# Cross-attention: keys, values and queries projected with tokens on partitions

## What is computed

```
q = layernorm(x) @ Wq + bq;  k = ctx @ Wk + bk;  v = ctx @ Wv + bv      # 256 -> 32 = 8 heads x 4
attn = softmax(q k^T * scale) per head;  o = attn v
x = x + tanh(g_xattn) * (o @ Wo + bo)
logits = layernorm(x) @ router_w + router_b;  scores = softmax(logits)  # 8 experts
per expert: the 512 tokens with the highest scores; relu(tok @ w1 + b1) @ w2 + b2, times score, added back
x = x + tanh(g_ffn) * (that sum)
```

## Time and profile before

| | |
|---|---|
| median of 3 runs | 587.21 us (587.1 to 587.39) |
| the profiled execution | 587.2 us, span 585.4 us |
| TensorE (PE) busy | 549.5 us, 94% |
| VectorE (DVE) | 443.0 us, 76% |
| ScalarE (ACT) | 389.7 us, 67% |
| GpSimd (POOL) | 215.3 us, 37% |

### The profile page before, as it was taken

One profiled execution on the slowest core, in us unless ns is written; L12 is line 12 of the kernel. 1 busy time (PEld: TensorE's weight loads), 2 busy tenths in 40 slices (PEclk: granted clock), 3 DMA queues, 4 the chain that ended last, 5 costly groups with the idle time before them and its releaser, 6 DMA issues.

```text
span 585.4 us, 12822 instructions
## 1 busy us (share of the span) xinstructions
PE 549.5 (94%) x5043; PEld 320.0 (55%) x5043; DVE 443.0 (76%) x811; ACT 389.7 (67%) x762; POOL 215.3 (37%) x205
## 2 busy tenths in 40 slices
PE   7799999999999999999999988899999999999994
PEld 3433333333343333433334444479889898898973
DVE  3889989998899878999895277655866858676541
ACT  1577878988789887898889820055665556555651
POOL 3057175001835018300157110231544625447234
PEclk9999999999999999999999999999999999999998
DMA  8700000000000000000000104113634646356133
GB/s 279 248 2 1 1 1 3 2 1 38 2 37 2 2 38 1 38 2 2 37 38 2 38 19 163 31 50 100 146 108 109 166 133 136 109 109 168 14 36 36
DMA packets 23808, 35.80 MB, mean 61 GB/s; under 512 B 3460, under 2 KB 16197, under 8 KB 23621
## 3 DMA queue, kind: packets, MB, share of 16 engines
q1 hardware_dynamic: 17604, 26.59, 13.9%
q0 software_dynamic: 6144, 8.39, 8.1%
HBM read 26.59 MB, written 8.39 MB: 60 GB/s over the span
## 4 chain that ended last, share of the span: by engine, by line
PE 71%; DVE 17%; ACT 4%; issue 4%; POOL 1%; DMA 1%; POOLq 0%; DVEq 0%; ACTq 0%; SPq 0%
PE ps L1744 15%; PE ps L1751 15%; PE ps L1515 13%; DVE mquart L1040 10%; PE ps L1481 7%; PE ps L1502 6%; ACT probs L767 2%; PE ps L1411 2%; PE ps L1372 2%; PE ps L1387 1%; PE ps L1722 1%; PE ps L1697 1%; ACT osb L666 1%; PE ps L1540 1%; POOL out L636 1%
## 5 line engine op out<-in xcount | busy, mean ns | idle before, releaser
L1040 DVE TENSOR_REDUCE mquart<-ps 128x2 f32<-128x802 f32 x256 | 240.1, 988 | 25.8 <-PE ps L1481 23.7
L767 ACT ACTIVATE probs<-ps 128x512 f32<-128x512 f32 (+1 forms) x416 | 223.4, 595 | 27.6 <-PE ps L1502 25.0
L1515 PE MATMUL ps<-probs,vp 128*32 128x256 f32 (+1 forms) x1664 | 132.7, 391 | 4.2 <-ACT osb L666 4.0
L1481 PE MATMUL ps<-kpad,qrows 64*128 64x401 bf16 x512 | 89.5, 337 | 5.5 <-DVE mquart L1040 5.2
L1502 PE MATMUL ps<-qfull,kpad 64*128 64x256 bf16 (+1 forms) x832 | 88.6, 272 | 1.6 <-ACT x L788 1.4
L1340 DVE TENSOR_TENSOR h1l<-hf,h1h 128x512 fp32r<-128x512 f32 x64 | 44.3, 692 | 56.0 <-ACT hf L892 48.0
L891 ACT ACTIVATE h1h<-ps,b1T 128x512 fp32r<-128x512 f32 x64 | 43.9, 686 | 54.3 <-PE ps L1744 52.5
L1751 PE MATMUL ps<-w2h,h1h 128*128 128x256 f32 x256 | 73.8, 288 | 2.1 <-DVE h1l L1340 1.5
L1751 PE MATMUL ps<-w2l,h1h 128*128 128x256 f32 x256 | 72.4, 283 | 0.0
L1751 PE MATMUL ps<-w2h,h1l 128*128 128x256 f32 x256 | 72.3, 283 | 0.0
L636 POOL DMA_INDIRECT out<-eo,idx_put x32 | 55.2, 1726 | 26.2 <-ACT eo L901 17.0
(11 more groups left out here) (200 smaller groups left out, 696.1 us busy)
## 6 DMA issues: line engine op xcount, KB each, us to landing
w1raw<-in_L_ffn_w SPq DMA_DIRECT2D x16, 512.0 KB, 4.6
w2raw<-in_L_ffn_w SPq DMA_DIRECT2D x16, 512.0 KB
xs<-in_x SPq DMA_DIRECT2D x4, 512.0 KB, 7.5
ctx_sb<-in_ctx SPq DMA_DIRECT2D x3, 512.0 KB, 5.8
out<-xs SPq DMA_DIRECT2D x3, 512.0 KB, 2.7
x_rows<-x SPq DMA_DIRECT2D x3, 512.0 KB, 2.6
b2b<-in_L_ffn_b SPq DMA_DIRECT2D x1, 1024.0 KB, 11.3
out<-xs SPq DMA_DIRECT2D x2, 256.0 KB, 2.0
```

What stands on the lines that cost most here:

```text
L767: nc.scalar.activation(out_p, ps[0:w, next_bank(), :], ACT.Exp, scale=float(SCALE)).then_inc(s_ex, 1)
L1040: nc.vector.tensor_reduce(mquart[:, u % 2, t, a, :, kq], ps[:, b:b + 2, 0:MAXW], AX.X, ALU.max).then_inc(s_mr, 1)
L1481: last = mm(ps[:, bank + b, 0:MAXW], qrows[band(b), g, q:q + P], kpad[band(b), g, a, lo:lo + MAXW], start=True, stop=True)
L1515: last = mm(ps[32 * hh:32 * hh + 32, PV, 0:UW], vp[0:w, kt, g, hh, :], probs[0:w, step % PROBS, hh, :], start=(kt == 0), stop=(kt == NKT - 1))
```

## The change

The f32 weights for keys and values lie side by side (`wkv_sb`, 64 columns). `project_kv` takes 128 context tokens as weights of the array and the 64 columns as moving data, so keys and values come out with tokens on partitions, for both groups at once; the bias is one product of a row of ones. ScalarE copies k and v to `kvsb` and writes the high part into two slots of `ktok` (`keys_high`), VectorE writes middle and low (`keys_split`), GpSimd the third high one and the values into `vp` (`high_again`). `turn_keys` multiplies a tile of `ktok` with the identity in bf16, which turns it to rows; the padded copies are made straight from PSUM (`pad_k0` by VectorE for blocks 0, 2, 3, by ScalarE for block 1; `pad_k1` by ScalarE).

For queries: `project_q`, then the split in `qtok` (by VectorE for chunk 0 in `first_queries`, by GpSimd for later chunks), `turn_q` for each group, and a copy to `qrows`. Per chunk there is one projection at (1, 3) and turns at (1, 7) and (1, 9). `max_parts` writes its two parts into `qtok` itself, and `place_max` turns `qtok` once more, maxima included, without the product that copied the rows. Replicated weights, bias products, four keep-busy products and the transposes of values go.

```diff
+KV_BANKS, TURN_BANKS, Q_BANK, QT_BANK = (4, 5, 4, 5), (2, 6, 2, 1), 3, 0
+kparts = ktok[:, :, :, :].rearrange("p n g (h j d) -> p (n g h) j d", j=8, d=HD)
+qparts = [qtok[:, i, :, :, :].rearrange("p t g (h j d) -> p (t g h) j d", j=8, d=HD) for i in range(2)]
+HEADS = CT * NH
...
-XN_FIRST, XN_LATER, Q_AT = ((0, 7), (0, 9)), ((0, 0), (0, 3)), ((1, 3), (1, 7))
+XN_FIRST, XN_LATER, Q_AT, ROWS_AT = ((0, 7), (0, 9)), ((0, 0), (0, 3)), (1, 3), ((1, 7), (1, 9))
...
-FIRST_VALUES, FIRST_KEYS, FIRST_QUERIES = (2, 6, 10, 13), (3, 7), 11
...
+FIRST_KEYS, FIRST_QUERIES = (1, 3, 5, 7), 9
...
-    for t, w in ((wk_sb, Wk), (wq_sb, Wq), (wv_sb, Wv)):
-        sp.dma_start(t[:, :, :], w.rearrange("(k p) n -> p k n", p=P)).then_inc(s_wts, 16)
+    for t, w in ((wkv_sb[:, :, 0:32], Wk), (wkv_sb[:, :, 32:64], Wv), (wq_sb[:, :, :], Wq)):
...
-    nc.gpsimd.memset(wqr[:, :, :, :], 0.0)
-    nc.gpsimd.memset(wkr[:, :, :, :], 0.0)
-    nc.gpsimd.memset(bqkr[:, :, :], 0.0).then_inc(s_zero, 1)
-    nc.gpsimd.memset(mparts[:, :, :, :], 0.0).then_inc(s_zero, 1)
+    nc.gpsimd.memset(ktok[:, :, :, :], 0.0).then_inc(s_zero, 1)
+    pool.wait_ge(s_zero, 1)
+    nc.gpsimd.memset(kparts[:, :, KROW_M // HD, 0:2], 1.0).then_inc(s_zero, 1)
+    nc.gpsimd.memset(qtok[:, :, :, :, :], 0.0).then_inc(s_zero, 1)
     nc.gpsimd.memset(vp[:, :, :, :, :], 0.0).then_inc(s_zero, 1)
-    pool.wait_ge(s_zero, 3)
+    pool.wait_ge(s_zero, 4)
...
+    def high_again(j):
+        ms, w = keys_of(j), block_rows(j)[1]
+        pool.wait_ge(s_khi, j + 1)
+        nc.gpsimd.tensor_copy(kparts[0:w, ms, 5, :], kparts[0:w, ms, 0, :]).then_inc(s_kh5, 1)
+        pool.wait_ge(s_zero, 5)
+        nc.gpsimd.tensor_copy(vp[:, :, :, :, :].rearrange("p k g h d -> p (k g h) d")[0:w, ms, 0:HD],
+                              kvsb[0:w, j % 2, P:P + 32 * (ms.stop - ms.start) // NH].rearrange("p (m d) -> p m d", d=HD)).then_inc(s_vp, 1)
...
-    for b, (lo, w) in enumerate(KB):
...
-    split_rest(pool, nc.gpsimd, 9, 1, CW)
-    split_rows(pool, nc.gpsimd, 9, CW, qrows[:, 1, 0:CW])
+    for j in range(4):
+        high_again(j)
...
-    def split_queries(c, g, n):
...
+    def split_queries(c):
+        parts, q = qparts[c % 2], qsb[:, :].rearrange("p (m d) -> p m d", d=HD)
+        rest = qres[:, :].rearrange("p (m d) -> p m d", d=HD)
+        pool.wait_ge(s_qtk, c)
+        if c > 1:
+            pool.wait_ge(s_mpl, PER_CHUNK * (c - 1))
+            nc.gpsimd.memset(parts[:, :, KROW_M // HD, 0:2], 0.0)
+        nc.gpsimd.tensor_copy(parts[:, :, 0:2, :], q.unsqueeze(2).to_broadcast([P, HEADS, 2, HD])).then_inc(s_qhi, 1)
+        pool.wait_ge(s_qhi, c)
+        nc.gpsimd.tensor_tensor(rest, q, parts[:, :, 0, :], ALU.subtract).then_inc(s_qrest, 1)
+        nc.gpsimd.tensor_copy(parts[:, :, 4, :], q)
+        pool.wait_ge(s_qrest, c)
+        nc.gpsimd.tensor_copy(parts[:, :, 2:4, :], rest.unsqueeze(2).to_broadcast([P, HEADS, 2, HD])).then_inc(s_qmid, 1)
+        pool.wait_ge(s_qmid, c)
+        nc.gpsimd.tensor_tensor(parts[:, :, 5, :], rest, parts[:, :, 2, :], ALU.subtract).then_inc(s_qd, 1)
...
-    def qk_bias(n, half, kind, g, w, bank, s_ready, cnt_ready):
...
+    def keys_high(j):
+        (tiles, w), ms = block_rows(j), keys_of(j)
+        act.wait_ge(s_kv, j + 1)
+        act.wait_ge(s_zero, 2)
+        if j > 1:
+            act.wait_ge(s_ktok, j - 1)
+            act.wait_ge(s_vp, j - 1)
+        nc.scalar.activation(kvsb[0:w, j % 2, :].rearrange("p (x c) -> p x c", x=2)[:, :, 0:32 * tiles],
+                             ps[0:w, KV_BANKS[j], 0:2 * P].rearrange("p (x c) -> p x c", x=2)[:, :, 0:32 * tiles], ACT.Copy)
+        nc.scalar.activation(kparts[0:w, ms, 0:4:2, :],
+                             ps[0:w, KV_BANKS[j], 0:32 * tiles].rearrange("p (m d) -> p m d", d=HD).unsqueeze(2).to_broadcast([w, NH * tiles, 2, HD]),
+                             ACT.Copy).then_inc(s_khi, 1)
+    def pad_k0(j):
+        lo, w = KB[j]
+        act.wait_ge(s_kt, j + 1)
+        for b in range(2):
+            last = nc.scalar.activation(kpad[:, 0, b, lo:lo + w], ps[:, TURN_BANKS[j], 0:w], ACT.Copy,
+                                        scale=cst[:, C_HEAD + b:C_HEAD + b + 1])
+        last.then_inc(s_ka, 1)
+    def take_q(c, g, bank):
+        act.wait_ge(s_qt, NG * c + g + 1)
+        take(qrows[:, g, CW * c:CW * c + CW], ps[:, bank, :], s_qr)
...
     take_ctx(0)
     take_ctx(1)
-    act.wait_ge(s_bias, 1)
-    bias_k(0)
+    keys_high(0)
     take_ctx(2)
-    bias_k(1)
-    take_v(0, 0)
+    keys_high(1)
     take_ctx(3)
-    bias_k(2)
     for k in range(KD):
         act.wait_ge(s_T, k + 1)
         take(xnT[:, k, :], ps[:, XN_BANKS[k], :], s_Tt)
-    take_v(1, 0)
-    bias_k(3)
-    qk_bias(4, 2, "q", 0, CW, JOB, s_Q, 1)
-    take_v(2, 0)
-    take_v(3, 0)
+    keys_high(2)
+    keys_high(3)
+    pad_k0(1)
+    take_q(0, 0, QT_BANK)
...
-        qk_bias(5 + j, (5 + j) % 2, "k", 1, KB[j][1], next_bank(), s_kp, 4 + j + 1)
...
+        pad_k1(j, next_bank())
+    take_q(0, 1, next_bank())
+    def take_q_tokens(c, bank):
+        act.wait_ge(s_Q, c + 1)
+        at_least(act, s_qd, c - 1)
+        take(qsb[:, :], ps[:, bank, 0:CW // HD], s_qtk)
...
-    for w, r in ((wk_sb, wkr), (wq_sb, wqr)):
...
-    def split(n, half, w, mask, dst):
...
     def keys_split(j):
+        (tiles, w), ms = block_rows(j), keys_of(j)
+        k, rest = [a.rearrange("p (m d) -> p m d", d=HD) for a in (kvsb[0:w, j % 2, 0:32 * tiles], kres[0:w, 0:32 * tiles])]
+        dve.wait_ge(s_khi, j + 1)
+        at_least(dve, s_ktok, j)
+        link(nc.vector.tensor_tensor(rest, k, kparts[0:w, ms, 0, :], ALU.subtract))
+        link(nc.vector.tensor_copy(kparts[0:w, ms, 1:5:2, :], rest.unsqueeze(2).to_broadcast([w, NH * tiles, 2, HD])))
+        nc.vector.tensor_tensor(kparts[0:w, ms, 4, :], rest, kparts[0:w, ms, 1, :], ALU.subtract).then_inc(s_ktok, 1)
+    def pad_k0(j):
         lo, w = KB[j]
-        split(j, j % 2, w, 2, krows[:, j % 2, 0:w])
-        dve.wait_ge(s_rows, j + 1)
+        dve.wait_ge(s_kt, j + 1)
         for b in range(2):
-            last = nc.vector.tensor_scalar(kpad[:, 0, b, lo:lo + w], krows[:, j % 2, 0:w],
-                                           cst[:, C_HEAD + b:C_HEAD + b + 1], None, ALU.mult)
-        last.then_inc(s_kpad0, 1)
+            last = nc.vector.tensor_scalar(kpad[:, 0, b, lo:lo + w], ps[:, TURN_BANKS[j], 0:w], cst[:, C_HEAD + b:C_HEAD + b + 1], None, ALU.mult)
+        last.then_inc(s_kd, 1)
+    def first_queries():
+        q, rest = [a.rearrange("p (m d) -> p m d", d=HD) for a in (ps[:, Q_BANK, 0:CW // HD], qres[:, :])]
+        parts = qparts[0]
+        dve.wait_ge(s_Q, 1)
+        link(nc.vector.tensor_copy(parts[:, :, 0:2, :], q.unsqueeze(2).to_broadcast([P, HEADS, 2, HD])))
+        link(nc.vector.tensor_tensor(rest, q, parts[:, :, 0, :], ALU.subtract))
+        nc.vector.tensor_copy(parts[:, :, 4, :], parts[:, :, 0, :])
+        link(nc.vector.tensor_copy(parts[:, :, 2:4, :], rest.unsqueeze(2).to_broadcast([P, HEADS, 2, HD])))
+        nc.vector.tensor_tensor(parts[:, :, 5, :], rest, parts[:, :, 2, :], ALU.subtract).then_inc(s_q0, 1)
     take_ctx(0)
     for t in range(CT):
         ln1_stats(0, t)
     take_ctx(1)
     ln1_aggr(0)
+    keys_split(0)
     take_ctx(2)
-    keys_split(0)
     ln1_apply_first()
+    keys_split(1)
     take_ctx(3)
-    keys_split(1)
+    pad_k0(0)
     keys_split(2)
     keys_split(3)
-    split(4, 2, CW, 0, qrows[:, 0, 0:CW])
+    first_queries()
+    pad_k0(2)
+    pad_k0(3)
...
-        at_least(dve, s_mpl, u)
-        def spread(t, row):
-            return t[:, :, :, row].rearrange("p t (b a) -> p t a b", a=2)
-        nc.vector.tensor_reduce(spread(mparts, KROW_M), mquart[:, u % 2, :, :, :, :], AX.X, ALU.max, negate=True)
+        c, g, h, r = unit(u)
+        placed = qtok[:, c % 2, UQ * h:UQ * h + UQ, g, :].rearrange("p t (h r) -> p t h r", r=32)
+        nc.vector.tensor_reduce(placed[:, :, :, KROW_M].rearrange("p t (b a) -> p t a b", a=2), mquart[:, u % 2, :, :, :, :], AX.X, ALU.max, negate=True)
         nc.vector.tensor_reduce(nmax[:, :, :].rearrange("p t (b a) -> p t a b", a=2), mquart[:, u % 2, :, :, :, :], AX.X, ALU.max,
                                 negate=True).then_inc(s_nm, 1)
         dve.wait_ge(s_nm, u + 1)
-        nc.vector.tensor_tensor(mparts[:, :, :, KROW_M + 1], nmax[:, :, :], mparts[:, :, :, KROW_M], ALU.subtract).then_inc(s_mp, 1)
+        nc.vector.tensor_tensor(placed[:, :, :, KROW_M + 1], nmax[:, :, :], placed[:, :, :, KROW_M], ALU.subtract).then_inc(s_mp, 1)
...
-    pe.wait_ge(s_wrep, 1)
-    for j in range(2 * NG):
-        last = mm(job[:, j:j + 1], bqkr[:, j, :], cst[0:1, C_ONE:C_ONE + 1], start=True, stop=True)
-    last.then_inc(s_biasp, 1)
-    keep_busy(4)
-    def k_project(j, g, bank, ks=range(KD)):
...
-    def transpose_v(j, g, bank=PV):
...
+    def project_kv(j):
+        (tiles, w), bank = block_rows(j), KV_BANKS[j]
+        if j == 0:
+            pe.wait_ge(s_wts, 96)
```

(99 more changed lines are left out.)

184 lines of the change are left out of this document (30 added, 154 removed).

## The result

The changed kernel takes 581.54 us, median of four runs (581.33 to 581.55); the kernel before took 587.15 beside it (four runs, 586.30 to 587.39). The ratio (time after by time before, with its 95% interval) is 0.9906 [0.9889, 0.9923]: faster by 5.6 us, where 8.0 were forecast. The profiled execution took 581.54 us, 1.8 more than its span.

A forecast was written before the change was run, and what follows sets the result against it. In attention TensorE was taken as the nearer bound, ahead of it a chain alternating between engines. Gains of 4.1 (start), 2.7 (query projections) and 1.2 (placing product) sum to 8.0: 587.2 to 579.2 us, own range 577 to 581.5, wider 575 to 584.

The forecast's parts named there:

- Start, first reduction: Ahead of attention: the first maximum's reduction starts at 28.25 instead of 30.42, behind VectorE's pads; 2.2 us gained.
- the straight line: VectorE's elementwise prices from 0.20 us for 32 elements and 0.69 for 512: 0.30 for 128, 0.43 for 256.
- Start, the sixteen reductions: End of the start: VectorE runs through the first sixteen reductions without waiting, ending at 43.3 instead of 47.42; 1.9 us gained here.
- Rival 2: Start: transposes begin at half clock, losing 0.5 to 1.9 us, 579.7 to 581.1; counted inside the forecast's 0.60.
- Query projections: Attention, three chunks: two projections, 3.84 us, become one and two turns, 2.95, on the bounding TensorE; 2.7 us gained.
- Placing product: Attention: the product placing query rows, 0.12 us, goes from every unit and counts in ten of fifteen; 1.2 us gained.
- GpSimd's split: Attention, turn at (1,7): the query split takes 3.5 us with waits, against 5.5 of cover; hidden by 2.
- Behind attention: Router and expert layers: untouched by the change, carried over at about 249.6 us; no gain or loss.
- Rival 1: Only one part pays: attention's 3.9 us go (583.1) or the start's 4.1 (583.3); chance 0.20 together with (4).
- Rivals 3 (slower, weight loads in series): Start and attention: weight load and columns don't overlap, 0.24 us per f32 record instead of 0.12; 593 us, chance 0.07.
- 4 (pads and turns late by GpSimd): Start: GpSimd's copies each over 1 us late through contention with VectorE, giving back 4.1 us; chance 0.20 with (1).
- Rival 5: Elementwise work is cheaper than priced and every unit yields its 0.12; two to three us more, 576.5; chance 0.10.

The follow-up runs named there:

- added products: Changed kernel with four products (eight f32 records) computed in vain ahead of each of the three later query projections: 587.71 us, ratio 1.0015 against the kernel before.

## Why the prediction was right or wrong

The measured 581.54 us stands at the upper edge of the forecast's own range (577 to 581.5), within 575 to 584. The saving is 5.6 of 8.0 us, by terms that came out as follows.

**Start, first reduction: right, 2.65 us for 2.2.** Transposes began at 9.39 (9.6 forecast), the token projection's records lie 0.12 apart as priced, the first reduction waited for VectorE's pads, as forecast; its product on TensorE, by then at half clock, ended only 0.04 us earlier. The query split was cheaper: 256 elements from SBUF take 0.29, as do 128, where the straight line gave 0.43, so it took 1.5 instead of 1.8; key splits 0.94 instead of 1.05. The pads from PSUM took 0.70 each (1.41 for two) against 0.31 from SBUF. That is what the sum took. The Trainium skill ("VectorE: DVE Perf Modes", section "Mode 2×_2P") says that the two-port mode needs SBUF. The two prices agree with it in direction, but don't show it by themselves, since the pads' source also changed from bf16 to f32.

**Start, the sixteen reductions: the step that failed was "VectorE runs through".** 15.05 us were forecast (28.25 to 43.3; its own terms add up to 15.14), 16.32 taken. VectorE does run through wherever the clock or the queue allowed it, in 14.74 to 14.76 us in six executions, 0.3 under the forecast. What the sum lacked is that TensorE would be at half clock here, and that the two keep-busy products in its queue between the tiles, 0.43 us each at that clock, would then delay the tiles that VectorE waits for. Rival 2 had the right mechanism at the wrong place: it put a half clock at the first transposes, which ran at nearly full rate (2.04 us for sixteen; 1.91 in two other executions). In two more executions they took 2.31 and 2.37, which fits its smaller price of half a microsecond; this varies without any edit to them. Rival 2 considered what is removed ahead of 9.6 us, and not what the new projections do to the clock later. The Trainium skill ("TensorE: Matmul & The Clock Gate", section "What's actually happening") states that activity releases the throttle. No row here contradicts that as such, but busy time in the profile didn't stand for it: the clock fell in windows in which TensorE's records fill 2.00 of 2.00 us.

**Query projections: right, 2.7 us for 2.7.** Units 1, 5 and 9 lost 0.88 to 0.90 us each. TensorE's bound in them is shown by the added products.

**Placing product: wrong, 0.1 us for 1.2.** The step was "in ten of fifteen units TensorE is ahead of VectorE in busy time or decides the unit". Busy time over a unit doesn't tell which wait ends last at the product's own place. The earlier trace rows carried that step, and no row was read of what ScalarE did at 86.43 to 86.75, though the rows shown above were there. The 0.1 lies in the last two units. The first unit was forecast unchanged and is 0.10 longer, because its first exponential starts earlier without the product and its end doesn't move; so the sum over attention lacks the whole 1.2.

**GpSimd's split: right in effect, wrong in size.** It took 2.2 us (143.23 to 145.39) where 3.5 were estimated, and is hidden by 1.8. The estimate scaled by elements a row of another form. That the cover is near the 2 forecast is luck. The four steps of 1.4 us between projection and turn are four of 1.1 (142.79 to 147.23, 4.4 us instead of 5.5), and the two errors nearly cancel.

**Behind attention: wrong by 0.4.** "Carried over as it is" missed 0.40 us. Of it 0.34 lie at the last half's residual, where VectorE starts 5.08 us behind the last exponential instead of 4.74. The products that it waits for start 3.9 us behind that exponential in both kernels, so the added time lies between them and VectorE's start (1.16 us instead of 0.81). Every variant has it, and none was made to separate it; its cause is open.

In sum 0.7 (start), 1.2 (attention) and 0.4 us (behind it) of the forecast were missing, 2.3, and 579.2 + 2.3 is the 581.5 measured. The start's 0.7 is a gain of 0.5 on the first reduction against a loss of 1.3 on the sixteen. Rival 1 (only one part pays, 583) has the placing product on its side and the query projections against it. Rivals 3 (slower, weight loads in series) and 4 (pads and turns late by GpSimd) found nothing: the records lie 0.12 apart, and the turn of keys at 17.42 follows without a wait. Rival 5 was right on the cheaper elementwise steps, 0.3 us, and wrong on its other half.

## What to carry to other kernels

When a change turns wide products on the bounding engine into many narrow ones, price the records (here an f32 record with 128-column weights cost 0.12 us with 32, 64 or 128 moving columns), and read the granted clock during and behind them. In the four executions in which the columns of the queries were filled with repeats, at 0.08 us per projection, the clock held at the start; that the kernel got faster by it isn't shown. A keep-busy product is work in the queue; at half clock it costs twice, and ahead of a product that another engine waits for it may cost more than it protects. Before counting a product taken from the busiest engine as gained, look at the very place: what does its consumer do at that moment?

## What the hardware showed that was not expected

- TensorE's granted clock fell to 0.50 at 23.6 to 26.6 us, during or up to 2.2 us behind 18 f32 records of 32 moving columns, in eight of eight executions. With 128 columns in the same records it held in four of four, even over 1.5 us of standstill. Yet in attention it held behind such records in 23 of 24 cases. The one fall there came after no gap in TensorE's records at all (144 to 150 us of the kernel with added products).
- Half clock by itself was nearly free where VectorE was the bound: 16 reductions took 14.76 us at 0.50 and 14.75 at 1.00, once no keep-busy product stood in TensorE's queue. The first exponential behind them came 0.5 us later.
- Widening 16 f32 records from 32 or 64 to 128 columns made them 0.05 to 0.08 us longer in all. With weights of 65 columns instead of 128 the price was not flat: the four records of the short block took 0.45 us with 64 moving columns and 0.65 with 128.
